# Writing the quantized FFN weights to memory already transposed, instead of transposing them at each load

## The reference

```
def _weight_quant(w):
    scale = 1.0 / clip(mean(abs(w)), 1e-05)
    return clip(round(w * scale), -1.0, 1.0) / scale
def _act_quant(x):
    scale = 127.0 / clip(max(abs(x), axis=-1), 1e-05)
    return clip(round(x * scale), -128.0, 127.0) / scale
def _bitlinear(x, w):                       # w is [out, in]
    return einsum('bsi,oi->bso', _act_quant(x), _weight_quant(w))

xn   = layernorm(x)
g, v, d = xn @ Wg + bg, xn @ Wv + bv, xn @ Wd + bd
scan = linear_scan(sigmoid(g) * tanh(v), a=0.001 + 0.998 * sigmoid(d))   # along the sequence
gate = silu(_bitlinear(xn, w_gate))         # w_gate [4096, 1024]
up   = _bitlinear(xn, w_up)                 # w_up   [4096, 1024]
out  = x + scan + _bitlinear(gate * up, w_down)     # w_down [1024, 4096]
```

## Time and profile before

| | |
|---|---|
| median of 3 runs | 6776.02 us |
| the profiled execution | 6789.32 us, its span on the slowest core (core 2) 6787.8 us |
| spans of the 8 cores | 6734.4 to 6787.8 us |
| TensorE busy | 2030.6 us, 30% of the span |
| VectorE busy | 2816.2 us, 41% |
| GpSimd busy | 1310.8 us, 19% |
| ScalarE busy | 395.7 us, 6% |
| weight preparation, all three | about 1701 to 3082 us of the span |
| B1 | 3176 to 5668 us |
| B2 | 5668 to 6788 us |

### The profile page before, as it was taken

One profiled execution on the slowest core, in us unless ns is written; L12 is line 12 of the kernel. 1 busy time (PEld: TensorE's weight loads), 2 busy tenths in 40 slices (PEclk: granted clock), 3 DMA queues, 4 the chain that ended last, 5 costly groups with the idle time before them and its releaser, 6 DMA issues.

```text
span 6787.8 us, 42054 instructions; the slowest of 8 cores (6734.4 to 6787.8 us)
## 1 busy us (share of the span) xinstructions
PE 2030.6 (30%) x9367; PEld 954.0 (14%) x9490; DVE 2816.2 (41%) x4453; ACT 395.7 (6%) x676; POOL 1310.8 (19%) x994
## 2 busy tenths in 40 slices
PE   0033333333000000002443344433344432545454
PEld 0022222222000000001111111111111110111111
DVE  2344444444433434331555555555555552010101
ACT  1111111111000000000000000000000000000000
POOL 0000000000021121220444434444344442000000
PEclk9966666666555555556776777777776666888888
DMA  3111111111422324225111111111111115889888
GB/s 87 65 41 38 44 44 44 44 39 40 131 63 76 125 70 133 68 70 113 30 30 30 36 29 29 30 30 30 36 29 30 30 30 129 175 183 180 178 190 175
DMA packets 944440, 504.33 MB, mean 74 GB/s; under 512 B 859136, under 2 KB 859168, under 8 KB 936000
## 3 DMA queue, kind: packets, MB, share of 16 engines
q1 hardware_dynamic: 940544, 495.22, 29.1%
q0 software_dynamic: 3648, 6.41, 0.6%
HBM read 197.25 MB, written 109.05 MB: 45 GB/s over the span
## 4 chain that ended last, share of the span: by engine, by line
DVE 34%; SPq 20%; DMA 17%; POOL 10%; issue 8%; PE 6%; ACT 2%; DVEq 1%; POOLq 0%; ACTq 0%
SPq L768 9%; SPq L641 4%; DVE qci L240 4%; DVE x_grp L242 4%; POOL pqstage L270 4%; DMA wqg<-scr_wd 3%; DVE x_grp L253 3%; DVE x_grp L251 3%; DMA pbuf<-wdown 3%; POOL x_grp L245 2%; DVE qg L510 2%; SPq L394 2%; DVE x_grp L265 2%; DVE x_grp L267 2%; DMA pbuf<-wup 2%
## 5 line engine op out<-in xcount | busy, mean ns | idle before, releaser
L665 PE MATMUL pb<-wqg,xqF_t 128*128 128x512 bf16 x1966 | 827.2, 421 | 1320.4 <-DMA xqF_t<-scr_xq 1137.6
L669 PE MATMUL pb<-wqu,xqF_t 128*128 128x512 bf16 x2048 | 858.8, 419 | 508.0 <-DMA xqF_t<-scr_xq 495.3
L270 POOL TENSOR_TENSOR pqstage<-x_grp 128x512 bf16<-128x512 f32 x192 | 264.9, 1380 | 2798.9 <-DVE x_grp L267 2798.9
L785 PE MATMUL pb<-wqg 128*128 128x512 bf16 x2007 | 545.8, 404 | 649.9 <-DMA wqg<-scr_wd 643.4
L442 PE MATMUL pb<-wqu,wqg 128*128 128x256 bf16 x3072 | 389.5, 289 | 1129.4 <-DMA wqu<-scr_xn 1129.4
L256 POOL TENSOR_TENSOR x_grp<-x_grp 128x512 f32<-128x512 f32 x256 | 378.3, 1478 | 1104.2 <-DVE x_grp L253 1104.2
L665 PEld LDWEIGHTS pb<-wqg,xqF_t 128*128 128x128 bf16 x2048 | 217.2, 106 | 2159.3 <-issue 1993.2
L442 PEld LDWEIGHTS pb<-wqu,wqg 128*128 128x128 bf16 x3072 | 311.1, 103 | 1184.1 <-issue 1132.6
L803 DVE TENSOR_SCALAR qt<-pb,dpwall 128x512 f32<-128x512 f32 x64 | 48.0, 751 | 1028.0 <-PE pb L785 1001.7
L696 DVE SCALAR_TENSOR_TENSOR pbuf<-pb,dvecs,epi 128x512 f32<-128x512 f32 x128 | 96.1, 750 | 750.9 <-ACT epi L679 741.1
L263 DVE TENSOR_SCALAR qt<-pbuf,wsc 128x512 f32<-128x512 f32 x192 | 94.4, 492 | 597.4 <-DMA pbuf<-wdown 214.9
(11 more groups left out here) (89 smaller groups left out, 2402.5 us busy)
## 6 DMA issues: line engine op xcount, KB each, us to landing
pbuf<-wdown SPq DMA_DIRECT2D x64, 512.0 KB, 5.0
pbuf<-wgate SPq DMA_DIRECT2D x64, 512.0 KB, 3.8
pbuf<-wup SPq DMA_DIRECT2D x64, 512.0 KB, 3.8
scr_pqF<-pqstage SPq DMA_DIRECT2D x32, 1024.0 KB, 3.9
wqg<-scr_pqF SPq DMA_DIRECT2D x32, 1024.0 KB, 8.3
pbuf<-x SPq DMA_DIRECT2D x32, 512.0 KB, 3.2
x_grp<-x SPq DMA_DIRECT2D x32, 512.0 KB, 5.1
pbuf<-scr_acc SPq DMA_DIRECT2D x32, 512.0 KB, 10.2
```

Source lines behind the costliest of these rows:

```text
L270: e.tensor_tensor(o, a, b, OP.subtract), wait=(vb,))
L665: e.matmul(o, l, r, start=st, stop=sp),
L669: e.matmul(o, l, r, start=st, stop=sp),
L785: e.matmul(o, l, r, start=st, stop=sp),
```

## The change

`prep_quant` now transposes each quantized chunk before it stores it. After the second half is rounded it calls `emit_xpose4` twice, which makes 8 DMA transposes of 128 x 128 from `pqstage` to `qtmp` (even chunks) or `pqroll` (odd chunks), and then issues 8 stores of 128 x 128 into the transposed scratch tensors `scr_wgT`, `scr_wuT` (1024 x 4096) and `scr_wdT` (4096 x 1024). The first of the 8 stores waits for both groups of transposes. A row of such a store is 256 bytes, where a row of the old store was 2048. Where the kernel needs the weights, it now loads them as they lie: 16 plain loads of 128 x 4096 in stage 4, and 512 plain loads of 128 x 1024 in B2. The two PSUM tensors `ptb0` and `ptb1`, which nothing used, became `pb6` and `pb7`, which nothing uses either. The rest is bookkeeping of waits: a slot of `pqstage` is written again when its transposes are done, and `qtmp` and `pqroll` when the stores that read them are done.

```diff
--- before.py
+++ after.py
@@ -52,9 +52,9 @@
     scr_xq = nc.dram_tensor("scr_xq", [T_TOK, D], BF16, kind="Internal").ap()
     scr_xn = nc.dram_tensor("scr_xn", [T_TOK, D], BF16, kind="Internal").ap()
     scr_pqF = nc.dram_tensor("scr_pqF", [NT, 128, INNER], BF16, kind="Internal").ap()
-    scr_wg = nc.dram_tensor("scr_wg", [INNER, D], BF16, kind="Internal").ap()
-    scr_wu = nc.dram_tensor("scr_wu", [INNER, D], BF16, kind="Internal").ap()
-    scr_wd = nc.dram_tensor("scr_wd", [D, INNER], BF16, kind="Internal").ap()
+    scr_wgT = nc.dram_tensor("scr_wgT", [D, INNER], BF16, kind="Internal").ap()
+    scr_wuT = nc.dram_tensor("scr_wuT", [D, INNER], BF16, kind="Internal").ap()
+    scr_wdT = nc.dram_tensor("scr_wdT", [INNER, D], BF16, kind="Internal").ap()
 
     es = ExitStack()
 
...
@@ -515,12 +514,14 @@
         def qtmp4(cc, c0, w):
             return pqstage[:, cc * D + c0:cc * D + c0 + w]
 
-        def prep_quant(load_list, sw_col, scr_nat, store_sem_unused, first_guard=()):
+        pq_state = {"slot_xp": {}, "xstage_st": {}, "prev_g": [None]}
+
+        def prep_quant(load_list, sw_col, first_guard=()):
             vmarks = {}
-            store_marks = {}
-            prev_g = [None]
-            sw0s = [wv(s4) for s4 in SWs]
-            for li, (src_slice, dst_rows) in enumerate(load_list):
+            prev_g = pq_state["prev_g"]
+            slot_xp = pq_state["slot_xp"]
+            xstage_st = pq_state["xstage_st"]
+            for li, (src_slice, dst_fn) in enumerate(load_list):
                 buf = wchunk[li % 4]
                 lp = LP[li % 4]
                 lw_ = (vmarks[li - 4],) if li >= 4 else (wv(V),)
@@ -530,10 +531,9 @@
                 gmark = None
                 for pc in range(2):
                     pw = [ldw] if pc == 0 else []
-                    if pc == 0 and li >= 4:
-                        pw.append(store_marks[li - 4])
-                    if pc == 0 and li < 4:
-                        pw.append(sw0s[li % 4])
+                    if pc == 0 and (li % 4) in slot_xp:
+                        pw.extend(slot_xp[li % 4])
+                    if pc == 0 and (li % 4) not in slot_xp:
                         pw.extend(first_guard)
                     bg = (prev_g[0],) if prev_g[0] is not None else ()
                     gmark = emit_round_neg_gw(buf[:, pc * 512:(pc + 1) * 512],
@@ -542,47 +542,64 @@
                                               pre_wait=tuple(pw), b_guard=bg)
                     prev_g[0] = gmark
                 vmarks[li] = wv(V)
-                op("y", lambda e, i_=qtmp4(li % 4, 0, D), o=dst_rows:
-                   e.dma_start(out=o, in_=i_), sem=SWs[li % 4], inc=16,
-                   wait=(gmark,))
-                store_marks[li] = wv(SWs[li % 4])
+                xst = qtmp if li % 2 == 0 else pqroll
+                xw = [gmark]
+                if (li % 2) in xstage_st:
+                    xw.append(xstage_st[li % 2])
+                for half in range(2):
+                    emit_xpose4([qtmp4(li % 4, half * 512 + b4 * 128, 128)
+                                 for b4 in range(4)],
+                                xst[:, half * 512:(half + 1) * 512],
+                                src_wait=tuple(xw))
+                slot_xp[li % 4] = last_xpose_marks(2)
+                for j in range(8):
+                    op("y", lambda e, i_=xst[:, j * 128:(j + 1) * 128], o=dst_fn(j):
+                       e.dma_start(out=o, in_=i_), sem=SWs[li % 4], inc=16,
+                       wait=slot_xp[li % 4] if j == 0 else ())
+                xstage_st[li % 2] = wv(SWs[li % 4])
 
         down_l1 = [d_wdown[c * 128:(c + 1) * 128, q * D:(q + 1) * D]
                    for c in range(8) for q in range(4)]
         prep_mean(down_l1)
         prep_scalars(4, 5, 1.0 / (D * INNER))
         down_l2 = [(d_wdown[c * 128:(c + 1) * 128, q * D:(q + 1) * D],
-                    scr_wd[c * 128:(c + 1) * 128, q * D:(q + 1) * D])
+                    (lambda j, c=c, q=q:
+                     scr_wdT[q * D + j * 128:q * D + (j + 1) * 128,
+                             c * 128:(c + 1) * 128]))
                    for c in range(8) for q in range(4)]
-        prep_quant(down_l2, 4, scr_wd, None, first_guard=((SX, sx_group[NG - 1]),))
+        prep_quant(down_l2, 4, first_guard=((SX, sx_group[NG - 1]),))
         st_wd = tuple(wv(s4) for s4 in SWs)
 
         gate_l1 = [d_wgate[c * 128:(c + 1) * 128, :] for c in range(32)]
         prep_mean(gate_l1)
         prep_scalars(0, 1, 1.0 / (INNER * D))
-        gate_l2 = [(d_wgate[c * 128:(c + 1) * 128, :], scr_wg[c * 128:(c + 1) * 128, :])
+        gate_l2 = [(d_wgate[c * 128:(c + 1) * 128, :],
+                    (lambda j, c=c:
+                     scr_wgT[j * 128:(j + 1) * 128, c * 128:(c + 1) * 128]))
                    for c in range(32)]
-        prep_quant(gate_l2, 0, scr_wg, None)
+        prep_quant(gate_l2, 0)
         st_wg = tuple(wv(s4) for s4 in SWs)
...
         last_attn_T = wv(T)
         for k in range(8):
             op("y", lambda e, o=wqg[:, k * INNER:(k + 1) * INNER],
-               i_=scr_wg[:, k * 128:(k + 1) * 128]:
-               e.dma_start_transpose(o, i_), sem=WT, inc=16,
+               i_=scr_wgT[k * 128:(k + 1) * 128, :]:
+               e.dma_start(out=o, in_=i_), sem=WT, inc=16,
                wait=(st_wg + (last_attn_T,)) if k == 0 else ())
         for k in range(8):
             op("y", lambda e, o=wqu[:, k * INNER:(k + 1) * INNER],
-               i_=scr_wu[:, k * 128:(k + 1) * 128]:
-               e.dma_start_transpose(o, i_), sem=WT, inc=16,
+               i_=scr_wuT[k * 128:(k + 1) * 128, :]:
+               e.dma_start(out=o, in_=i_), sem=WT, inc=16,
                wait=(st_wu + (last_attn_T, (SN, sn_group[NG - 1]))) if k == 0 else ())
         wt_done = wv(WT)
 
@@ -619,8 +636,15 @@
                                      scal[:, 1:2], pc % 2,
                                      qt_guard=qg, pre_wait=tuple(pw))
 
+        prep_roll_guard = {0: pq_state["xstage_st"].get(1),
+                           1: pq_state["xstage_st"].get(1),
+                           2: pq_state["xstage_st"].get(0),
+                           3: pq_state["xstage_st"].get(0)}
+
         def b1_tail(ti, pc):
             bg = (gfin[(ti, pc - 1)],) if (ti, pc - 1) in gfin else                  ((gfin[(ti - 1, 7)],) if (ti - 1, 7) in gfin else ())
+            if ti == 0 and pc < 4 and prep_roll_guard[pc] is not None:
+                bg = bg + (prep_roll_guard[pc],)
             gfin[(ti, pc)] = gq_tail(gqs[(ti, pc)], roll[pc % 4], b_guard=bg)
 
         def b1_store(ti):
@@ -764,8 +788,8 @@
                     w_wait.append((T, t_k_mark[(uu, kk)]))
                 else:
                     w_wait.append(b1_done_T)
-                op("y", lambda e, o=wbuf, i_=scr_wd[:, k * 128:(k + 1) * 128]:
-                   e.dma_start_transpose(o, i_),
+                op("y", lambda e, o=wbuf, i_=scr_wdT[k * 128:(k + 1) * 128, :]:
+                   e.dma_start(out=o, in_=i_),
                    sem=lw, inc=16, wait=tuple(w_wait))
                 ld_w = wv(lw)
                 for j in range(2):
```

More of the change, by code:

```diff
@@ L141, in wdT_str @@
             return wqg[:, 8192 + j * D:8192 + (j + 1) * D]
-        pb = [ps(f"pb{i}", [128, 512], F32) for i in range(6)]
-        ptb = [ps("ptb0", [128, 1024], BF16), ps("ptb1", [128, 1024], BF16)]
+        pb = [ps(f"pb{i}", [128, 512], F32) for i in range(8)]
         names = ["G", "T", "V", "S", "LA0", "LX0", "LX1", "LP0", "LP1",
@@ L570, in build_program @@
         prep_scalars(2, 3, 1.0 / (INNER * D))
-        up_l2 = [(d_wup[c * 128:(c + 1) * 128, :], scr_wu[c * 128:(c + 1) * 128, :])
+        up_l2 = [(d_wup[c * 128:(c + 1) * 128, :],
+                  (lambda j, c=c:
+                   scr_wuT[j * 128:(j + 1) * 128, c * 128:(c + 1) * 128]))
                  for c in range(32)]
-        prep_quant(up_l2, 2, scr_wu, None)
+        prep_quant(up_l2, 2)
         st_wu = tuple(wv(s4) for s4 in SWs)
```

## The result

The changed kernel takes 7854.99 us (median of 8 runs, 7830.5 to 7866.72) against 6777.75 us (8 runs) for the kernel before: 1.1589 times as long, 95% interval 1.1574 to 1.1604. Forecast were 8000 us, 1.18 times, within 7780 to 8310. The direction and the mechanism were right; the cost was put 145 us too high. The transposes in the preparation were priced 139 us too high and B2's gain 33 us too low (mean of the cores), while the stores were priced 29 us too low.

What follows compares the result with a forecast made beforehand. Quantization was taken as a chain of waits with nothing full, B2 as paced by its DMA transposes. 6789 + 1507 - 37 - 248 = 8011, less 13 for the profiled execution, rounded to 8000 us; range 7780 to 8310.

Steps and rivals of the forecast that it cites:

- The tail of a chunk: In quantization, transposes, landing and stores before the next load on SyncE's list add 15.7 us per turn, 96 times: 1507 us.
- 8 transposes, taken at 11.5 us: Per chunk in quantization, issuing eight 128 x 128 transposes on SyncE adds 11.5 us, between 10.4 and 11.8.
- The landing, taken at 1.2 us: Per chunk in quantization, the wait for the last transpose to land adds 1.2 us, between 1.0 and 1.4.
- Seven stores, taken at 3.0 us: Per chunk in quantization, seven more stores at 0.43 us of issue each add 3.0 us, between 2.3 and 3.5.
- The load behind the stores, taken at 0: In quantization, the next load queued behind eight stores of 256-byte rows is not delayed; upper bound 11 us.
- Weight loads, taken at 37 us less: Ahead of B1, 16.8 MB loaded plainly bring the first matmul 37 us earlier, between 25 and 45.
- B2, taken at 248 us less: In B2, plain loads cut each of 16 supertiles from 70 to 54.5 us, 248 us less in all.
- The 2 us for TensorE and the DMAs not fitting together: In a B2 supertile, 2 us added because TensorE's end at 43 and the DMAs' at 42 are so near.
- The first: Rival: in quantization the 256-byte stores hold up the load behind them, 288 us more, 8288 us; chance 0.09.
- The second: Rival: in B2 plain slices of 2 KB rows come no faster than the transposes, 8283 us; chance 0.09.
- The third: Rival: in the quiet preparation a transpose is issued like a plain DMA, 0.43 us, giving 7288 us; chance 0.04.
- The fourth: Rival: in quantization the tail runs under the next chunk's load and rounding; wholly hidden, 6491 us; chance 0.01.

## Why the prediction was right, and where its terms were off

- **The tail of a chunk stands in series, 96 times.** Shown: on core 2 the turns grew from 12.25 us (w_down) and 11.35 (the others) to 26.5 and 26.0, and loads issued ahead gave 1028 us back.
- **8 transposes, taken at 11.5 us, measured 10.0 to 10.06, below the 10.4 that was the lower bound.** This is the term that was mis-sized most. The row of 11.28 us in the earlier trace rows is a merged row, and there was a wait in it: the same eight, asked for in two narrow windows of the kernel before, are

```profile
4351.63 4.92 SPq L284 DMA_TRANSPOSE pqstage<-qtmp  x4
...
4357.99 4.92 SPq L284 DMA_TRANSPOSE pqstage<-qtmp  x4
```

  so from 4356.55 to 4357.99 SyncE was waiting for GpSimd's next piece (L258, which ended at 4357.87). The median of the earlier trace rows, 8 x 1.232 = 9.9 us, would have given the price but for 0.2 us; I explained its distance to the merged row as gaps. 96 x 1.45 = 139 us. In that row "x8" counts what stands on the list in a row, not what ran without a pause.
- **The landing, taken at 1.2 us.** 1.2 (4463.58 to 4464.74).
- **Seven stores, taken at 3.0 us.** 3.66 - 0.34 = 3.3 us, 96 x 0.3 = 29 us too little. Not held up by the length of their rows, as taken.
- **The load behind the stores, taken at 0.** It is 0: the medians from its issue to its reader are 4.4 us (w_down) and 3.9 (w_gate) on core 2 with eight stores ahead, 4.5 and 3.9 before.
- Together a turn grew on core 2 by 14.25 (w_down) and 14.7 us, 1397 us over 96, where 1507 were forecast. A weight took 31 turns in 811 to 822 us, so 836 to 848 in all, under the 860 that the prediction named at least.
- **Weight loads, taken at 37 us less.** First matmul 56.2 us after the first load's issue (core 6) where 56 were worked out, 37 less than before on core 2. Core by core it is 36 to 41 less. The DMAs were full (share 0.99) at 323 GB/s.
- **B2, taken at 248 us less.** 296, from the first matmul to the end on core 2 (7032.5 to 7838.5, before 5685.8 to 6787.8). Core by core it is 256 (core 6) to 302, 281 in the mean. The stretch of 30 us was right. The 2 us for TensorE and the DMAs not fitting together were not needed: with 244 GB/s at a share of 0.80 the slices stay ahead, as the window of the second stretch shows.

```profile
7110.00:7140.00 30.00, 29.76 (x128) 12.83 (x126) 0.07 (x1) 0.00 (x0) 0.00 (x0) 0.93 0.80 244
```

  The boundary took 7.7 us (7087.78 to 7095.50) where I had taken the one of the earlier trace rows, 9.2. That one was the longest of core 2, whose others took 7.7 to 9.1, while on core 6 they took 7.7 to 8.05 before the change too; in it VectorE waited 0.9 and 1.2 us for output stores, in the new one 0.6. TensorE's start took 14.3 us from the issue of the loads (7095.50 to 7109.77), not 13.3. On core 6 some luck helped: the supertile was taken too long both before (70 for 68.1) and after (54.5 for 52.2), and the difference came out near the 256 us measured.
- **The rule that transposing DMAs are as fast as plain ones** ("Advanced Engine Details and Errata", X-Bar Transpose, in the Trainium skill) does not hold here: the same 16 loads of 1 MB moved 206 GB/s with the transpose and 323 without, both with full DMAs.
- **The rivals.** The first is answered by the eight stores above. The second would have left the stretch of B2 at 47 us; it is 30.3. The third would have the transposes issued in 0.43 us each in the quiet preparation; the median of the 768 there is 1.23 us, and the least 1.09. The fourth is answered by the loads issued ahead.

On core 2 the terms measured give 1397 - 37 - 296 = 1064; its span grew by 7838.5 - 6787.8 = 1051, with B1 6 us shorter. Over the eight cores the mean span grew by 1079 and the medians of the runs by 1077.

## What to carry to other kernels

Work moved from a stage that repeats it to a stage that does it once pays only if it is priced where it lands: 8 small DMAs that are nothing beside a bound engine cost their full issue time when the next load stands behind them on the same list. Before adding to such a list, take the loads out of the series; it was worth more here (456 us) than the plain loads bring (331 us). With the loads ahead and one store per chunk, transposes on an idle TensorE came free; no run has them without the loads ahead. Price an issue by its single instances, not by a merged row, which can hold a wait. And before taking a length from one instance, look at the others, and at a second core.

## What the runs showed of the hardware

- The issue of a DMA on SyncE costs nearly the same for 128 rows of 2 KB, 128 rows of 256 bytes and 1024 rows of 256 bytes (0.34, 0.43 and 0.38 us); a transpose of 128 x 128 costs 1.23 us.
- The issue can take longer behind many bytes in flight: behind 16 plain loads of 1 MB the 16 input transposes kept SyncE's queue for 39.72 us, a single one for up to 10.4, where they took 20.77 behind transposes. What it waits for in the queue is not shown.
- 256 KB written in rows of 256 bytes land 2.8 us after their issue (one store per chunk), in rows of 2 KB 2.2 us (w_gate and w_up before). For w_down it is 2.8 to 2.9 against 2.8. The 32 KB stores of the changed kernel land after 1.5 to 1.6 us. So short rows cost little in this quiet stage; the runs don't show what they would cost beside full DMAs.
